# Gated cross attention with a routed layer: context rows with room for eight columns, and the turned weights in two buffers of their own

## The chip, the cores and the metric

The kernel runs on one core of a Trainium2 chip. The metric is the device time of one execution in microseconds (us); less is better. The time of a version is the median of its runs.

## The reference

`x` is (32, 112, 512), the context `ctx_2048` is (32, 375, 512), all fp32. For each of the 32 batches the kernel computes one head of attention over the context, and then every token goes to the one of eight experts that a router picks.

```python
def attend(h, memory, mask):                  # (B,112,512), (B,375,512), (B,375)
    scores = einsum('bsd,bmd->bsm', h, memory) / sqrt(512)
    scores = where(mask[:, None, :], scores, -1e30)
    return einsum('bsm,bmd->bsd', softmax(scores), memory)   # 0 where no row is valid

def routed(x, Wg, W, b):
    probs = softmax(x @ Wg)                   # 8 experts
    e = argmax(probs)
    return probs[e] * (x @ W[e] + b[e])

x = x + tanh(g_xattn) * attend(layernorm(x), ctx_2048, mask)
x = x + tanh(g_ffn) * routed(layernorm(x), Wg, W, b)
```

## The kernel before

The work has two phases. In the **batch phase** a loop goes over the 32 batches (unrolled by four, `TURN = 4`), software pipelined: each engine's program for step i works on several batches at once. In the **tail phase** 35 tiles of 128 tokens, sorted by expert, are gathered, multiplied with their expert's matrix and scattered to the output.

*Layout.* The 375 rows of a context are put on 125 partitions (`MP`), three rows each (`MC = 3`): partition p holds rows 3p, 3p+1 and 3p+2, which adjoin in DRAM. In SBUF they lie in `ctx_sb`, shape (128, 12, 632): four slots (batches j, j+1, j+2, j+3) of three chunks, and each chunk has `SE + D` = 120 + 512 columns. The 512 are the context row. The 120 (`SE`) are in front of it, for the turned softmax weights: `S` = 112 columns for the tokens of the batch and `E` = 8 for the router's part. A chunk is then, in one row of SBUF, [112 weights | 8 router values | 512 context values].

*SP (sync)* issues the loads. In `batch(i)` (line 393) it waits for `w_lo_ok`, loads a piece of the expert matrices (`load_w`, line 373), waits for `x2_ok` of batch i, stores batch i's rows to DRAM (`mid_rows`, line 398) and issues `load(i + 4)`: x (line 366), then the context in two DMAs, partitions 0 to 111 (line 368) and 112 to 124 (line 369). Both count on one semaphore per slot, `ctx_ld`.

*TensorE (PE)* goes in step i, in this order (`batch`, line 1193): scores of batch i+1 (lines 1104 to 1108, the last being the mask matmul); the turn (transpose) of the softmax weights of batch i into `prob_ps` (`turn_weights`, line 1116); the turn of the context of batch i+2, quarters 0 and 1 (`ctx_turn`, line 1082), which waits for that batch's load; the router's ranks of batch i-2 (lines 1127 and 1128); the first third of the read-out of batch i (`read_out`, lines 1141 and 1142), the one that waits for `prT_ok`; the turn of x of batch i+2 (line 1091) and of the context's quarters 2 and 3; the other two thirds of the read-out. One third of a read-out is a matmul with 125x112 weights and 8 + 256 moving columns, and one with the other 256. The eight columns are the router's part, which the matmul multiplies with the softmax weights in the same pass.

*ScalarE (ACT)* goes in step i (`batch`, line 698): `apply1` (line 695), a small exponential for the router (line 712), `turned_weights` (line 680), then the copies of the turned context quarters out of PSUM (`ctx_part`, lines 630 and 632), of the turned x (line 687), of a piece of the matrices (line 742), and the softmax exponential (line 665).

*VectorE (DVE)* subtracts for the low parts of the fp32 split (lines 968 and 1053), takes the statistics of x of batch i+3 (`stats1`, line 769, which waits for that load), writes x2 (`residual`, line 824) and does the router's small steps. `read_counts` (line 942) reads a count that PE puts in unused columns of `prob_ps`, so it waits for `prT_ok` too.

*Tail phase.* `ctx_sb`'s 512-column parts are used again: eight chunks for the biases, four for the results (line 253), which GpSimd scatters (line 590).

`prT_ok` counts the copies of the turned weights, one a batch; `read_mm` counts finished read-outs.

Of the kernel before, what the change touches and what calls it, by code (L numbers as in the profile page):

```python
# [24 lines left out]
ACT = mybir.ActivationFunctionType  # L25
AX = mybir.AxisListType

P = 128
# [62 lines left out]
def loop_end(last):  # L91

    return (last - 4) // TURN * TURN
# [14 lines left out]
def build(nc, x, ctx, mask, small, w_exp, b_exp, out):  # L108
    B, S, D = x.shape
    M = ctx.shape[1]  # L110
    E = b_exp.shape[0]
    N = B * S
    KC = D // P
    MC = 3
    MP = M // MC

    MAIN = MP // 16 * 16
    ME = M + M % 2

    SE, MG = S + E, ME + E  # L120
# [3 lines left out]
    HALF = D // 2  # L124
# [7 lines left out]
    TAIL = loop_end(B + 2)  # L132
# [13 lines left out]
    with ExitStack() as stack:  # L146
        def sb(name, shape, dt=F32):
            return stack.enter_context(nc.sbuf_tensor(name, shape, dt))

        def ps(name):  # L150
            return stack.enter_context(nc.psum_tensor(name, [P, 512], F32))

        def sem(name):
            return stack.enter_context(nc.semaphore(name))


        ident = sb("ident", [P, P])
# [17 lines left out]
        late = w_lo[:, (B - 2) * D:B * D]  # L175
# [11 lines left out]
        gv = sb("gv", [P, B])  # L187

        x_sb = sb("x_sb", [P, 4, D])
        ctx_sb = sb("ctx_sb", [P, 4 * MC, SE + D])  # L190
        xn = sb("xn", [S, D])
        xnT_hi = sb("xnT_hi", [P, KS, SE], F32R)
        xnT_lo = sb("xnT_lo", [P, KS, SE], F32R)
# [56 lines left out]
        put = sb("put", [P, 4], U32)  # L250


        rows, biases, res = x_sb, ctx_sb[:, 0:E, SE:], ctx_sb[:, E:E + 4, SE:]
        rn = w_raw
        rnT_hi, rnT_lo = (part[:, :, :].rearrange("p k m -> p (k m)")[:, 0:2 * D].rearrange("p (a d) -> p a d", a=2)
                          for part in (ctxT_hi, ctxT_lo))
# [4 lines left out]
        read_a, read_b = read_both[0:S, 512 - HALF - E:512], read_both[0:S, 512:512 + HALF]  # L261
        read_ps, pg_ps = read_both[0:S, 512 - HALF:512 + HALF], read_both[0:S, 512 - HALF - E:512 - HALF]
        prob_ps = ps("prob_ps")
# [10 lines left out]
        def chunks(j):  # L274
            return slice(MC * j.slot(4), MC * j.slot(4) + MC)
# [6 lines left out]
        ctx_ld = [sem(f"ctx_ld{i}") for i in range(4)]  # L282
# [21 lines left out]
        prT_mm, prT_ok, read_mm = sem("prT_mm"), sem("prT_ok"), sem("read_mm")  # L304
# [59 lines left out]
        def _(sp):  # L364
            def load(j):
                sp.dma_start(x_sb[0:S, j.slot(4), :], x_rows[bass.ds(j.times(S), S), :]).then_inc(x_ld[j.slot(4)], 16)
                rows_of = ctx[bass.ds(j.times(1), 1), :, :].rearrange("o (p c) d -> p (o c) d", c=MC)
                sp.dma_start(ctx_sb[0:MAIN, chunks(j), SE:], rows_of[0:MAIN, :, :]).then_inc(ctx_ld[j.slot(4)], 16)
                sp.dma_start(ctx_sb[MAIN:MP, chunks(j), SE:], rows_of[MAIN:MP, :, :]).then_inc(ctx_ld[j.slot(4)], 16)

            def load_w(w):

# [245 lines left out]
        def _(act):  # L618
# [56 lines left out]

            def turned_weights(j):
                act.wait_ge(prT_mm, j.times(1, 1))
                if j.at_least(4):
                    act.wait_ge(read_mm, j.times(1, -3))
                act.activation(ctx_sb[0:MP, chunks(j), 0:SE],  # L680
                               prob_ps[0:MP, 0:MC * SE].rearrange("p (c s) -> p c s", c=MC), ACT.Copy).then_inc(prT_ok, 1)

            def turned_x(j):
                act.wait_ge(xnT_mm, j.times(1, 1))
# [68 lines left out]
        def _(dve):  # L753
# [187 lines left out]

            def read_counts(late):
                dve.wait_ge(count_mm, late + 1)
                dve.wait_ge(prT_ok, B if late else TAIL + 1)
                dve.tensor_scalar(cnt_i[:, :], count_ps, float(P - 1) if late else 0.0, None, ALU.add
                                  ).then_inc(count_ok, 1)
                dve.wait_ge(count_ok, 2 * late + 1)
                dve.tensor_scalar(til_i[:, :], cnt_i[:, :], 7, None, ALU.arith_shift_right).then_inc(count_ok, 1)
# [121 lines left out]
        def _(pe):  # L1070
            def ctx_turn(j, k):

                if k == 0:
                    pe.wait_ge(ctx_ld[j.slot(4)], j.rounds(4) * 32 + 32)
                if k >= 2:
                    pe.wait_ge(ctxT_ok, j.times(KS, k - 1))
                elif k == 1 and j.at_least(1):
                    pe.wait_ge(ctxT_full_ok, j.times(1))
                elif j.at_least(1):
                    pe.wait_ge(ctxT_ok, j.times(KS))  # L1080
                for c in range(MC):
                    last = pe.transpose(ctx_ps[k % 2][:, c * MP:(c + 1) * MP],  # L1082
                                        ctx_sb[0:MP, MC * j.slot(4) + c, SE + k * P:SE + (k + 1) * P], ident[0:MP, 0:MP])
                    if c == MC - 1:
                        last.then_inc(ctxT_mm, 1)

# [43 lines left out]
            def read_out(j, c):  # L1130
                a = j.slot(2)
                if c == 0:
                    pe.wait_ge(prT_ok, j.times(1, 1))
                    if j.at_least(1):
                        pe.wait_ge(x2_ok, j.times(1))
                        pe.wait_ge(lg_ok, j.times(1))
                    else:
                        pe.wait_ge(gv_ok, 1)

                turned = ctx_sb[0:MP, MC * j.slot(4) + c, :]  # L1140
                pe.matmul(read_a, turned[:, 0:S], turned[:, S:SE + HALF], start=(c == 0), stop=(c == MC - 1))  # L1141
                last = pe.matmul(read_b, turned[:, 0:S], turned[:, SE + HALF:], start=(c == 0), stop=(c == MC - 1))  # L1142
                if c == MC - 1:
                    last.then_inc(read_mm, 1)

# [159 lines left out]
```

## Time and profile before

| | us |
|---|---|
| median of 3 runs | 391.55 (391.52 to 391.95) |
| the profiled execution | 394.58 |
| its span, first to last instruction | 392.8 |
| PE busy | 359.2 (91%) |
| weight loads (PEld) busy | 302.1 (77%) |
| DVE busy | 301.0 (77%) |
| GpSimd (POOL) busy | 226.8 (58%) |
| ACT busy | 220.6 (56%) |
| HBM read, written | 51.68 MB, 17.10 MB |
| DMA packets | 39438, 67.21 MB |

A profile is one execution. Matmuls are pipelined, and their ends are modelled, so a busy PE need not be at its peak. The idle time of an engine is put down to whatever released it. The chain of waits is followed back from the last instruction, at each step to what released it; it shows which work ended last. The mean granted clock of TensorE is 0.976.

### The profile page before, as it was taken

The page shows a single profiled execution, that of the slowest core. Times are in us where ns is not written, and L with a number is a line of the kernel's source. Part 1 is how long each engine was busy: PE and PEld are TensorE (multiplying, and loading weights), DVE is VectorE, ACT ScalarE, POOL GpSimd, SP SyncE. Part 2 cuts the span into 40 slices and gives each one's busy share as a digit, 9 for nine tenths or more (in the row PEclk, how much of TensorE's full clock was granted, in tenths as well). Part 3 has the DMA queues.
Part 4 walks back from the last instruction along what each step waited for, and adds up shares of the span by engine and source line. Part 5 has one row for each costly group of instructions (what it writes and reads, how often), then busy time and mean ns, then how long its engine had stood idle before and what let it go on. Part 6 is the DMA issues. An engine that isn't in the chain of part 4 may idle for free.

```text
span 392.8 us, 9753 instructions
## 1 busy us (share of the span) xinstructions
PE 359.2 (91%) x2062; PEld 302.1 (77%) x2063; DVE 301.0 (77%) x1087; ACT 220.6 (56%) x488; POOL 226.8 (58%) x482
## 2 busy tenths in 40 slices
PE   7799999999999999999999999376999999999980
PEld 6688888878888888888888877255777878878760
DVE  4668888889898899889899988446877767767660
ACT  3577777777777677767777665132434444444410
POOL 5154675665666666665675654726466666666631
PEclk9999999999999999999999999968999999999995
DMA  7978789888989888899999861754345444445410
GB/s 197 222 188 222 179 196 221 194 199 204 202 203 197 206 193 217 201 188 220 198 201 234 196 152 52 164 179 135 110 158 158 141 146 145 129 149 158 153 37 0
DMA packets 39438, 67.21 MB, mean 171 GB/s; under 512 B 10578, under 2 KB 11094, under 8 KB 39416
## 3 DMA queue, kind: packets, MB, share of 16 engines
q1 hardware_dynamic: 32600, 50.35, 54.7%
q0 software_dynamic: 6624, 16.58, 13.2%
q8 instruction: 8, 0.13, 0.1%
q14 instruction: 14, 0.11, 0.1%
q10 hardware_dynamic: 192, 0.03, 0.0%
HBM read 51.68 MB, written 17.10 MB: 175 GB/s over the span
## 4 chain that ended last, share of the span: by engine, by line
PE 52%; DMA 16%; issue 9%; DVE 7%; POOL 6%; ACT 3%; SPq 3%; POOLq 1%; DVEq 1%; ACTq 0%
DMA ctx_sb<-in_ctx 8%; PE read_both L1141 8%; PE ctx_ps L1082 8%; PE read_both L1142 7%; DMA x_sb<-mid_rows,take 6%; PE score_ps L1180 4%; PE score_ps L1107 3%; POOL out_rows L590 3%; PE score_ps L1182 3%; PE score_ps L1181 3%; PE score_ps L1104 3%; PE score_ps L1105 3%; PE score_ps L1106 3%; PE prob_ps L1091 2%; PE ctx_ps L1162 2%
## 5 line engine op out<-in xcount | busy, mean ns | idle before, releaser
L1141 PE MATMUL read_both<-ctx_sb 125*112 125x264 f32 x192 | 61.1, 400 | 1.9 <-DVE lg L837 1.6
L1180 PE MATMUL score_ps<-w_hi,ctxT_hi 128*128 x140 | 59.7, 426 | 1.6 <-DVE ctxT_lo L908 1.6
L968 DVE TENSOR_TENSOR ctxT_lo<-ctx_ps,ctxT_hi 128x375 fp32r<-128x375 f32 x96 | 49.3, 541 | 13.2 <-ACT ctxT_hi L630 12.6
L520 POOL DMA_INDIRECT token_list<-pay,pos x32 | 32.2, 1007 | 46.2 <-DVE pos L889 41.1
L1142 PE MATMUL read_both<-ctx_sb 125*112 125x256 f32 x192 | 57.1, 379 | 0.0
L1082 PE MATMUL ctx_ps<-ident,ctx_sb 125*128 125x125 f32 x384 | 52.6, 272 | 4.4 <-DMA ctx_sb<-in_ctx 2.6
L1182 PE MATMUL score_ps<-w_lo,ctxT_hi 128*128 x140 | 56.4, 403 | 0.0
L1181 PE MATMUL score_ps<-w_hi,ctxT_lo 128*128 x140 | 56.3, 402 | 0.0
L581 POOL DMA_INDIRECT x_sb<-mid_rows,take x35 | 34.4, 982 | 29.8 <-DVE ctx_sb L926 17.9
L590 POOL DMA_INDIRECT out_rows<-ctx_sb,put x35 | 40.0, 1144 | 17.5 <-issue 9.4
L641 ACT ACTIVATE w_raw<-x_sb,li 128x512 f32<-128x512 f32 x35 | 28.5, 815 | 36.9 <-DMA x_sb<-mid_rows,take 36.9
L1082 PEld LDWEIGHTS ctx_ps<-ident,ctx_sb 125*128 125x128 f32 x384 | 42.4, 141 | 7.0 <-DMA ctx_sb<-in_ctx 2.7
L630 ACT ACTIVATE ctxT_hi<-ctx_ps 128x375 fp32r<-128x375 f32 x96 | 42.6, 481 | 4.9 <-PE ctx_ps L1082 4.9
L695 ACT ACTIVATE xn<-x_sb,ln 112x512 f32<-112x512 f32 x32 | 26.0, 814 | 33.3 <-POOL ln L484 33.3
L654 ACT ACTIVATE ctxT_hi<-ctx_ps 128x512 fp32r<-128x512 f32 x35 | 20.9, 598 | 40.6 <-PE ctx_ps L1162 40.6
L469 POOL TENSOR_TENSOR w_lo<-w_raw,w_hi 128x512 f32 (+1 forms) x32 | 40.8, 1275 | 0.0
L1142 PEld LDWEIGHTS read_both<-ctx_sb 125*112 125x112 f32 x192 | 34.0, 177 | 8.7
L1104 PE MATMUL score_ps<-ctxT_hi,xnT_hi 128*120 128x384 f32 x96 | 37.9, 395 | 1.8 <-DVE ctxT_lo L968 1.8
L921 DVE SCALAR_TENSOR_TENSOR x_sb<-ctx_sb,li,x_sb 128x512 f32<-128x512 f32 x35 | 26.3, 752 | 13.1 <-issue 12.8
L908 DVE TENSOR_TENSOR ctxT_lo<-ctx_ps,ctxT_hi 128x512 fp32r<-128x512 f32 x35 | 24.2, 691 | 15.1 <-ACT ctxT_hi L654 15.0
L1141 PEld LDWEIGHTS read_both<-ctx_sb 125*112 125x112 f32 x192 | 29.3, 176 | 5.3 <-ACT ctx_sb L680 2.3
L926 DVE SCALAR_TENSOR_TENSOR ctx_sb<-score_ps,li,x_sb 128x512 f32<-128x512 f32 x35 | 26.3, 751 | 8.7 <-PE score_ps L1182 7.7
(141 smaller groups left out, 828.2 us busy)
## 6 DMA issues: line engine op xcount, KB each, us to landing
ctx_sb<-in_ctx SPq DMA_DIRECT2D x32, 672.0 KB
w_raw<-in_L_ffn_W SPq DMA_DIRECT2D x32, 256.0 KB, 5.1
x_sb<-in_x SPq DMA_DIRECT2D x32, 224.0 KB, 4.4
mid_rows<-x SPq DMA_DIRECT2D x32, 224.0 KB, 3.4
ctx_sb<-in_ctx SPq DMA_DIRECT2D x32, 78.0 KB
ctx_sb<-in_L_ffn_b SPq DMA_DIRECT2D x8, 256.0 KB, 7.6
li<-token_list SPq DMA_DIRECT2D x35, 2.0 KB, 1.9
x_sb<-mid_rows,take POOLq DMA_INDIRECT x35, 3.4
```

What stands on the lines that cost most here:

```text
L469: pool.tensor_tensor(w_lo[:, bass.ds(w.times(D), D)], w_raw[:, w.slot(2), :], w_hi[:, bass.ds(w.times(D), D)].bitcast(F32), ALU.subtract). ...
L581: pool.indirect_dma_start(rows[:, b, :], None, source, bass.IndirectOffsetOnAxis(take[:, b:b + 1], 0)).then_inc(row_ld[b], 16)
L590: pool.indirect_dma_start(out, bass.IndirectOffsetOnAxis(put[:, b:b + 1], 0), res[:, b, :], None, bounds_check=N - 1, oob_is_err=False).th ...
L630: act.activation(ctxT_hi[:, k, 0:M], ctx_ps[k % 2][:, 0:M], ACT.Copy).then_inc(ctxT_hi_ok, 1)
L968: dve.tensor_tensor(ctxT_lo[:, k, 0:M], ctx_ps[k % 2][:, 0:M], ctxT_hi[:, k, 0:M].bitcast(F32), ALU.subtract).then_inc(ctxT_ok, 1)
L1082: last = pe.transpose(ctx_ps[k % 2][:, c * MP:(c + 1) * MP], ctx_sb[0:MP, MC * j.slot(4) + c, SE + k * P:SE + (k + 1) * P], ident[0:MP, 0:MP])
L1104: pe.matmul(score_ps[a][0:SE, 0:MG], xnT_hi[:, k, :], ctxT_hi[:, k, :], start=(k == 0), stop=False)
L1141: pe.matmul(read_a, turned[:, 0:S], turned[:, S:SE + HALF], start=(c == 0), stop=(c == MC - 1))
L1142: last = pe.matmul(read_b, turned[:, 0:S], turned[:, SE + HALF:], start=(c == 0), stop=(c == MC - 1))
L1180: pe.matmul(y_ps[a][:, :], hi, w_hi[:, chunk], start=(k == 0), stop=False)
L1181: pe.matmul(y_ps[a][:, :], lo, w_hi[:, chunk], start=False, stop=False)
L1182: last = pe.matmul(y_ps[a][:, :], hi, w_lo[:, chunk], start=False, stop=(k == KC - 1))
```

## The change

The context is given to the kernel with 8 (`E`) columns of zeros ahead of each row, so a row in DRAM has 520 columns, 2080 B; this is done on the host. `ctx_sb` has 520 columns a chunk: [8 router values | 512 context values]. A load writes all 520, so that the three rows of a partition are 1560 adjoining values on both sides, 6240 B. The router's values are written over the eight zeros later.

The 112 columns of turned weights move to a new tile, `turned`, with two buffers. `turned_weights` makes two copies in place of one: 125 x (3 x 112) to `turned`, and 125 x (3 x 8) to `ctx_sb`. `prT_ok` counts both, so that its waits ask for twice as much; the wait for `read_mm`, from the third batch on, asks for all read-outs but that of the batch just before. The read-out takes its weights from `turned` and its moving columns from `ctx_sb`. All other users of `ctx_sb` change their offset only.

```diff
@@ buffers
-        ctx_sb = sb("ctx_sb", [P, 4 * MC, SE + D])
+        ctx_sb = sb("ctx_sb", [P, 4 * MC, E + D])
+        turned = sb("turned", [P, 2, MC * S])
...
-        rows, biases, res = x_sb, ctx_sb[:, 0:E, SE:], ctx_sb[:, E:E + 4, SE:]
+        rows, biases, res = x_sb, ctx_sb[:, 0:E, E:], ctx_sb[:, E:E + 4, E:]
@@ sync, load(j)
-                sp.dma_start(ctx_sb[0:MAIN, chunks(j), SE:], rows_of[0:MAIN, :, :]).then_inc(ctx_ld[j.slot(4)], 16)
-                sp.dma_start(ctx_sb[MAIN:MP, chunks(j), SE:], rows_of[MAIN:MP, :, :]).then_inc(ctx_ld[j.slot(4)], 16)
+                sp.dma_start(ctx_sb[0:MAIN, chunks(j), :], rows_of[0:MAIN, :, :]).then_inc(ctx_ld[j.slot(4)], 16)
+                sp.dma_start(ctx_sb[MAIN:MP, chunks(j), :], rows_of[MAIN:MP, :, :]).then_inc(ctx_ld[j.slot(4)], 16)
@@ scalar, turned_weights(j)
                 act.wait_ge(prT_mm, j.times(1, 1))
-                if j.at_least(4):
-                    act.wait_ge(read_mm, j.times(1, -3))
-                act.activation(ctx_sb[0:MP, chunks(j), 0:SE],
-                               prob_ps[0:MP, 0:MC * SE].rearrange("p (c s) -> p c s", c=MC), ACT.Copy).then_inc(prT_ok, 1)
+                if j.at_least(2):
+                    act.wait_ge(read_mm, j.times(1, -1))
+                both = prob_ps[0:MP, 0:MC * SE].rearrange("p (c s) -> p c s", c=MC)
+                act.activation(turned[0:MP, j.slot(2), :].rearrange("p (c s) -> p c s", c=MC), both[:, :, 0:S], ACT.Copy
+                               ).then_inc(prT_ok, 1)
+                act.activation(ctx_sb[0:MP, chunks(j), 0:E], both[:, :, S:SE], ACT.Copy).then_inc(prT_ok, 1)
@@ vector, read_counts(late)
-                dve.wait_ge(prT_ok, B if late else TAIL + 1)
+                dve.wait_ge(prT_ok, 2 * (B if late else TAIL + 1))
@@ tensor, ctx_turn(j, k)
-                                        ctx_sb[0:MP, MC * j.slot(4) + c, SE + k * P:SE + (k + 1) * P], ident[0:MP, 0:MP])
+                                        ctx_sb[0:MP, MC * j.slot(4) + c, E + k * P:E + (k + 1) * P], ident[0:MP, 0:MP])
@@ tensor, read_out(j, c)
-                    pe.wait_ge(prT_ok, j.times(1, 1))
+                    pe.wait_ge(prT_ok, j.times(2, 2))
...
-                turned = ctx_sb[0:MP, MC * j.slot(4) + c, :]
-                pe.matmul(read_a, turned[:, 0:S], turned[:, S:SE + HALF], start=(c == 0), stop=(c == MC - 1))
-                last = pe.matmul(read_b, turned[:, 0:S], turned[:, SE + HALF:], start=(c == 0), stop=(c == MC - 1))
+                weight, values = turned[0:MP, a, c * S:(c + 1) * S], ctx_sb[0:MP, MC * j.slot(4) + c, :]
+                pe.matmul(read_a, weight, values[:, 0:E + HALF], start=(c == 0), stop=(c == MC - 1))
+                last = pe.matmul(read_b, weight, values[:, E + HALF:], start=(c == 0), stop=(c == MC - 1))
@@ host, kernel(**inputs)
+        if name == "ctx_2048":
+            room = inputs["L0_ffn_b"].shape[0]
+            a = _np.concatenate([_np.zeros(a.shape[:2] + (room,), a.dtype), a], axis=2)
```

## Rows read from the trace of the kernel before

**Rows 1.** Page, busy times; window 27.5 to 225.1 us, engines in that order.

```profile
PE 359.2 (91%) x2062; PEld 302.1 (77%) x2063; DVE 301.0 (77%) x1087; ACT 220.6 (56%) x488; POOL 226.8 (58%) x482
...
27.50:225.10 197.60, 195.78 (x1215) 170.28 (x1213) 176.03 (x719) 142.74 (x350) 124.27 (x323) 1.00 0.88 204
```

**Rows 2.** Chain of waits, 100 to 132 us: start us, us, what.

```profile
101.16 0.16 PE score_ps L1108
101.32 0.32 PE prob_ps L1116 x3
101.64 0.64 PE ctx_ps L1082 x6
...
102.34 0.56 PE read_both L1141 x2
102.90 0.43 PE read_both L1142 x2
...
104.36 0.45 PE read_both L1141 x2
...
108.33 0.16 PE score_ps L1108
...
115.59 0.16 PE score_ps L1108
```

**Rows 3.** Instructions of line 1108 on PE, 27 to 226 us.

```profile
L1108 PE MATMUL score_ps<-mask_add,ident_bf x28: 322/322/323, 27.5 to 225.1; 128*112 128x375 bf16 x28
```

**Rows 4.** Timeline of ACT, then of the weight loads, 101 to 103 us.

```profile
101.68 0.47 ACT L680 ACTIVATE ctx_sb<-prob_ps 125x360 f32<-125x360 f32 x1
102.05 0.85 ACT L630 ACTIVATE ctxT_hi<-ctx_ps 128x375 fp32r<-128x375 f32 x2
...
102.20 0.27 PEld L1141 LDWEIGHTS read_both<-ctx_sb 125*112 125x112 f32 x2
```

**Rows 5.** Groups of ACT by form: line, shapes, count | busy us, mean ns | idle.

```profile
L630 ACT ACTIVATE ctxT_hi<-ctx_ps 128x375 fp32r<-128x375 f32 x96 | 42.6, 481 | 4.9 <-PE ctx_ps L1082 4.9
...
L654 ACT ACTIVATE ctxT_hi<-ctx_ps 128x512 fp32r<-128x512 f32 x35 | 20.9, 598 | 40.6 <-PE ctx_ps L1162 40.6
...
L687 ACT ACTIVATE xnT_hi<-prob_ps 128x336 fp32r<-128x336 f32 x32 | 14.4, 451 | 25.9 <-PE prob_ps L1091 25.9
L712 ACT ACTIVATE lexp<-lsh,pay 112x8 f32<-112x8 f32 x32 | 9.3, 290 | 3.7 <-DVE lsh L862 3.7
```

**Rows 6.** DMA queues in windows 118.5:119.5, 300:380 and 27:225 us.

```profile
DMA packets 176, 0.36 MB, mean 360 GB/s; under 512 B 0, under 2 KB 0, under 8 KB 176
...
q1 hardware_dynamic: 176, 0.36, 100.0%
...
q0 software_dynamic: 3840, 11.28, 43.6%
...
q1 hardware_dynamic: 21714, 40.22, 87.7%
```

**Rows 7.** Timeline of SP's queue, 78 to 87 us: start us, us.

```profile
78.59 0.33 SPq L366 DMA_DIRECT2D x_sb<-in_x  x1
79.12 0.64 SPq L368 DMA_DIRECT2D ctx_sb<-in_ctx  x1
79.95 0.89 SPq L369 DMA_DIRECT2D ctx_sb<-in_ctx  x1
```

**Rows 8.** Waits of PEld, 27 to 226 us, then of DVE, 20 to 226 us.

```profile
PEld ctx_ps L1082 <- DMA ctx_sb<-in_ctx: 2.7, 5, 1.0
...
DVE st L769 <- DMA x_sb<-in_x: 1.3, 4, 0.5
```

**Rows 9.** Chain of waits, the context loads on it: start us, us, what.

```profile
2.03 6.01 DMA ctx_sb<-in_ctx
...
8.18 0.53 PE ctx_ps L1082 x3
...
79.95 7.12 DMA ctx_sb<-in_ctx
...
131.44 6.57 DMA ctx_sb<-in_ctx
```
## The prediction, made before the change was run

> **What bounds the kernel now.** I read the profile from coarse to fine: the shares of busy time, one steady stretch, the chain of waits over a few batches, the waits of TensorE's weight loads, then the DMA issues and landings. The sum below is made against one profiled execution: 394.58 us with a span of 392.8 us, which is 3.0 us above the 391.55 us median of the plain runs. I add the difference that I find to the median.
>
> TensorE (PE) is busy 91% of the span and ScalarE (ACT) 56%; from 27.5 to 225.1 us, where 27 batches pass, PE is busy 195.8 of 197.6 us at a granted clock of 1.00, while the 16 DMA engines are busy 88% at 204 GB/s [rows 1]. So two resources are nearly full at once. The chain of waits says which one ends last: between the mask matmuls of two neighbouring batches, from 101.16 to 108.33 us, it stays on PE throughout, and the period is 7.17 us; the next is 7.26 us [rows 2]. The mask matmul runs once a batch, 28 times from 27.5 to 225.1 us [rows 3]: 27 periods in 197.6 us, mean 7.32. Against the undisturbed 7.17 (193.6 us) that leaves 4.0 us lost in the stretch. That 4.0 us, and what the first load costs, is all that faster context loads can give back.
>
> Within a clean batch there is one place where PE waits on ACT. Its first pair of read-out matmuls (line 1141) takes 0.56 us on the chain, the next pair 0.45 us [rows 2]. The time in between is ACT's copy of the turned weights (line 680): it runs 101.68 to 102.15 us and the weight load behind it starts at 102.20 us [rows 4]. So the end of that copy already sets when the read-out begins, by 0.11 us per batch, and whatever ends later there goes straight onto the period.
>
> **The change, part by part.**
>
> 1. *The copy is split in two (ACT).* Today one copy of 125x360; then one of 125x336 into `turned` and one of 125x24 into `ctx_sb`, and PE waits for both (the count asked for is 2j+2). Price from the copies of the profile: 128x375 takes 481 ns, 128x512 takes 598 ns [rows 5], so 0.85 ns a column and 161 ns fixed. That gives 448 ns for 336 columns (line 687, with 336 columns, shows 451 [rows 5]) and 181 ns for 24. ACT overlaps neighbours: line 680 starts at 101.68 and runs 0.47, line 630 starts at 102.05, an overlap of 0.10 us [rows 4]. So the first copy ends 20 ns sooner and the second 80 ns after it: the weights are ready 60 ns later. The upper end is the small exponential of line 712 (112x8, 290 ns [rows 5]): 290 - 100 - 20 = 170 ns later. The lower end is 0.03 us; nothing or a gain is excluded, since a second instruction has to end after the first. I take 0.07 us, near the copies, which are the same kind of operation. PE waits at that place in about 30 of the 32 batches: +2.1 us (ends +0.9 and +5.1). ACT itself has room (142.7 us busy of 197.6 [rows 1]), and the copies of `ctx_ps` behind it slip by the same 0.07 us together with the PE work that needs them.
>
> 2. *The wait for `read_mm` becomes j-1 for j-3.* ACT has already waited for the turn of the weights of batch j, which PE issues after all read-outs of j-1. So the wait is always met: cost nothing; behind it stand the copies of `ctx_ps`, and they lose nothing.
>
> 3. *The context load.* Today 375 pieces of 2048 B a batch (112 and 13 partitions, three rows each), 23.4 for each of 16 DMA engines. After, a partition's three rows adjoin on both sides, one piece of 6240 B: 125 pieces, 7.8 for each engine, and 1.6% more bytes. In the fullest microsecond of a batch 176 packets of 2 KB pass in 16 engine-microseconds, 91 ns each, or 22.5 B/ns [rows 6]. If all of that were per packet, 15.6 fewer packets would save 1.4 us of a batch; if all of it were per byte, the load would take 0.03 us more. The row to decide between these ends is the gather and scatter queue of the tail: 3840 packets with a mean of 2.9 KB, 11.28 MB in 43.6% of 16 x 80 us, which is 20.2 B/ns [rows 6]. Its larger packets are no cheaper per byte than 22.5, so the part per packet is small. I take 0.2 us earlier, nearer the lower end, and keep both ends for the range. That the mean over the steady stretch is much worse (40.22 MB in 87.7% of 16 x 198 us, 14.5 B/ns [rows 6]) says that most of the time is waiting of another kind, and there the size of a piece may or may not help.
>
>  Here the Trainium skill speaks against the change: "DMA: Bandwidth & Descriptors", section "How a descriptor splits into AXI transactions", says that a read which does not start on a 256 B boundary fetches from the boundary below, and that those bytes cost beats. By that rule 6240 B rows, whose starts are spread over the multiples of 32 B, would cost 3.5 beats of 32 B on the mean over their 195, where today's reads start aligned: the load would then grow by 3.4% and not 1.6%, an estimate, and the sum would be 0.04 us a batch worse. No row of the trace shows a misaligned read from memory.
>
> 4. *SP's issue.* The main context issue takes 0.64 us for 336 pieces, the x issue 0.33 us for 112 [rows 7]. With 112 pieces it should take about 0.34, so SP is 0.3 us ahead for the tail issue (0.89 us today [rows 7]). The tail's packets stand behind those of the main load, so I count nothing for it. The weight load after it waits for GpSimd's subtraction, not for SP.
>
> 5. *What an earlier landing is worth.* In the steady stretch weight loads of line 1082 wait 2.7 us for context, in 5 places, and VectorE waits 1.3 us for x, in 4 [rows 8]. The other waits for context are nil because the loads arrive just in time: issue to landing takes 6 to 7 us of a 7.17 us period (6.01 at the start, 7.12 and 6.57 later [rows 9]). 0.2 us earlier gives 0.2 at each of the 5 places, 1.0 us; the x loads stand behind the weight load of the batch before, so some of it reaches them too: 0.2 us; and the first load, which nothing covers (landing 8.04, first turn 8.18 [rows 9]), gives 0.2 us. Sum -1.4 us. Ends: 0.03 us later at the same places, +0.2 us; and all of it back, -4.0 and some 0.8 at the start, -4.8.
>
> 6. *Tail phase.* Biases and results sit in `ctx_sb` at another pitch; the same rows of 2 KB are read and written. Nothing.
>
> Sum: +2.1 - 1.4 = +0.7 us, 392.3 us (395.3 for a profiled execution like that of before).
>
> **The rivals.**
>
> *Slower: the second copy is not a cheap follower.* Place: between the turn of the weights and the first read-out. Price: 0.17 us a batch, as line 712 has it, x 30 = +5.1, less 1.2 of part 5: 395.5 us. It decides from 0.1 us a batch on. For it: PE already waits exactly here. Against: the copies from PSUM follow a straight line in the number of columns down to 336.
>
> *Faster: the long pieces take most of the waiting out of the queue.* If context lands 0.8 us earlier, all 4.0 us of the steady stretch and 0.8 of the start come back: -4.8 + 2.1 = -2.7, 388.9 us; with 0.5 us it is about 389.8. For it: 14.5 against 22.5 B/ns, so there is waiting to remove. Against: the packets of the fullest microsecond show no cost that a longer piece would spare [rows 6], and the waiting between them need not come from their size.
>
> *Slower: odd starts make the loads longer.* Landings have little margin, so 0.25 us more would stall most batches, by perhaps 0.15 us each: +4.1 + 2.1, 397.7 us. This is the direction in which the skill's rule on 256 B points, but its own 0.04 us a batch would give only 1.1 us in 27 batches.
>
> *The change does not do what it says:* if the pieces stay one row each (2080 B), the load is 1.6% longer and only ACT's cost remains: 393.8 us.
>
> **How the numbers follow.** 0.2% is 0.8 us, about what a measurement of this kernel can tell from no change: faster is below 390.8, slower above 392.3. Forecast case (cost and gain nearly cancel, 391.2 to 393.2): 0.42. Faster rival: 0.25. Dear copy: 0.17. Longer loads: 0.08. No longer pieces: 0.08. Faster than 0.2%: 0.24 of the faster rival and 0.04 of the forecast case, 0.28. Within: 0.25 of the forecast case and 0.05 of the others, 0.30. Slower: 0.42. The forecast's own number stands at the edge of two of these. The range goes from 389.0 (nearly all of the faster rival) to 395.8 (the dear copy in it); it leaves out the longer loads and the last of the faster rival.
>
> **What would show it.** In the profile after: a first copy of about 448 ns and a second of 180 to 200 ns, the weight load of the read-out 0.05 us behind the end of the second, and clean periods of 7.22 to 7.25 us for 7.17. About 8,000 packets fewer on the hardware queue with 1% more bytes. Context landing 0.2 us sooner after its issue than in the rows of before, SP's main issue near 0.34 us. Waits for context in the steady stretch of about 1.5 us for 2.7. I am wrong if the clean period doesn't move (the copy is hidden), if it moves by over 0.12 us, or if the landing moves by over 0.5 us either way.

## The result, and the profile after

The changed kernel takes 394.5 us (median of 6 runs, 393.35 to 395.95) against 391.53 us before: ratio 1.0076, 95% interval 1.0043 to 1.0109. It is slower by 3.0 us.

The profiled executions don't show it: 394.83 us after and 394.58 us before, spans 393.0 and 392.8 us. The one of before lay 3 us above its median, so what it lost in waits must be weighed with care. But the two traces show clearly what changed.

The page and the window of the same 27 batches, from the mask matmul of batch 2 to that of batch 29 (29.7 to 225.4 us here), columns as in [rows 1]:

```profile
PE 360.8 (92%) x2062; PEld 304.4 (77%) x2063; DVE 300.0 (76%) x1087; ACT 222.6 (57%) x520; POOL 226.8 (58%) x482
...
29.70:225.40 195.70, 195.70 (x1215) 171.32 (x1213) 175.09 (x719) 144.29 (x377) 124.29 (x323) 1.00 0.83 208
```

PE is busy without a gap: 195.7 of 195.7 us, where it had 195.8 of 197.6. 27 periods take 195.7 us for 197.6. The chain of waits over three batches, start, length and what, against [rows 2]:

```profile
102.33 0.16 PE score_ps L1111
...
103.51 0.62 PE read_both L1144 x2
...
105.59 0.45 PE read_both L1144 x2
...
109.57 0.16 PE score_ps L1111
...
116.85 0.16 PE score_ps L1111
```

The period without a stall, the clean period, is 7.24 us for 7.17 (the smallest distance of two mask matmuls in the window is 7.23 for 7.16). The first pair of read-out matmuls takes 0.62 us where it took 0.56, the next pair 0.45 as before. ACT's timeline and the weight loads at that place, against [rows 4]:

```profile
102.85 0.45 ACT L682 ACTIVATE turned<-prob_ps 125x336 f32<-125x336 f32 x1
103.19 0.18 ACT L684 ACTIVATE ctx_sb<-prob_ps 125x24 f32<-125x24 f32 x1
103.26 0.87 ACT L631 ACTIVATE ctxT_hi<-ctx_ps 128x375 fp32r<-128x375 f32 x2
...
103.43 0.27 PEld L1144 LDWEIGHTS read_both<-ctx_sb,turned 125*112 125x112 f32 x2
```

The first copy takes 0.45 us and would let the read-out begin at 103.35. The second begins at 103.19, ends 185 ns later, at 103.38, and the weight load follows at 103.43, 0.05 us behind it.

The queues of the page and of the window 29 to 227 us, and SP's issues, against [rows 6, 7]:

```profile
DMA packets 15955, 40.98 MB, mean 207 GB/s; under 512 B 2927, under 2 KB 2927, under 8 KB 15944
...
q1 hardware_dynamic: 15112, 40.82, 82.2%
...
87.99 0.32 SPq L369 DMA_DIRECT2D ctx_sb<-in_ctx  x1
88.50 0.32 SPq L370 DMA_DIRECT2D ctx_sb<-in_ctx  x1
```

6,600 packets fewer carry 1.5% more bytes in 82.2% of the engines' time for 87.7%: 15.7 B/ns for 14.5. SP's context issues take 0.32 us each for 0.64 and 0.89. The context itself lands, by the trace's landing records, a median of 6.9 us after its main issue, for 7.2. The waits for context of [rows 8] are gone from this window, and the wait for x too.

The start tells the other half. Chain of waits, 0 to 18 us, against [rows 9]:

```profile
1.26 6.25 DMA small_sb<-in_small
...
7.54 0.22 DVE wg_part L786
...
8.67 1.18 PE score_ps L1267 x16
9.85 1.25 PE ctx_ps L1085 x6
...
16.33 0.16 PE score_ps L1111
```

Before, the chain ran through the first context load, which landed at 8.04 us. Now it runs through `small_sb`, the 17 KB of router weights and gates that ACT loads at the same time. Landing of that load before, and after:

```profile
DMA to landing us min/median/max: 2.6/2.6/2.6
...
DMA to landing us min/median/max: 6.3/6.3/6.3
```

It was issued at 1.3 us in both. From 1.5 to 5.5 us its queue's packets took 5.4% of the engines' time, for 4.8%, which is 0.2 us for each engine in both: the 3.7 us more lie between the packets, not in them. PE's program has the router's sum ahead of the first turn of a context, and the sum needs this load. The context itself landed at 7.7 us, but its first turn began at 9.64 us (8.18 before), and the first mask matmul came at 16.17 us for 14.03. TensorE stood idle for 2.4 us meanwhile, and its granted clock fell. PE's timeline at the router's sum, then windows of before and after, granted clock third from the end:

```profile
7.89 0.36 PE L1255 MATMUL small_ps<-wg_part,w_lo 128*128 128x8 f32 x2 [2.39 <-DVE wg_part L786]
...
8.00:14.00 6.00, 4.47 (x27) 3.64 (x28) 2.93 (x7) 2.53 (x6) 1.75 (x9) 1.00 0.90 233
...
8.00:16.20 8.20, 7.33 (x48) 6.38 (x49) 4.36 (x17) 3.29 (x7) 1.49 (x9) 0.79 0.67 170
```

So from trace to trace: +2.1 us at the start, +1.9 in 27 batches from the copies, -3.8 from stalls that are gone (what 27 periods take above 27 clean ones: 4.2 us before, with 7.16 us as the clean one, and 0.4 now). That makes +0.2 us, as the two spans have it, and not the +3.0 us of the medians.

The page's DMA issues, KB and median us to landing:

```profile
w_raw<-in_L_ffn_W SPq DMA_DIRECT2D x32, 256.0 KB, 4.6
x_sb<-in_x SPq DMA_DIRECT2D x32, 224.0 KB, 3.9
mid_rows<-x SPq DMA_DIRECT2D x32, 224.0 KB, 2.9
```

Before they took 5.1, 4.4 and 3.4 us. Each lands 0.5 us sooner after its issue, though only the context's pieces were changed. They stand in the same queue as the context; whether the longer pieces or the longer period shortened it, these two traces can't tell (see e1 and e5).

### The profile page after: what moved, and what is told of

Same layout as the page of the kernel before. It is cut to its first block, busy times and chain, and to the rows that moved or that the text cites. A ratio compares the mean times of both kernels' runs of the same rounds, so it can differ in the third digit from the quotient of the medians.

```text
span 393.0 us, 9811 instructions
## 1 busy us (share of the span) xinstructions
PE 360.8 (92%) x2062; PEld 304.4 (77%) x2063; DVE 300.0 (76%) x1087; ACT 222.6 (57%) x520; POOL 226.8 (58%) x482
## 4 chain that ended last, share of the span: by engine, by line
PE 80%; DMA 7%; DVE 4%; issue 3%; ACT 2%; POOL 1%; DVEq 0%; POOLq 0%; SPq 0%; ACTq 0%
PE read_both L1144 12%; PE ctx_ps L1085 10%; PE read_both L1145 10%; PE score_ps L1183 7%; PE score_ps L1185 6%; PE score_ps L1184 6%; DMA x_sb<-mid_rows,take 5%; PE score_ps L1110 5%; PE score_ps L1107 4%; PE score_ps L1108 4%; PE score_ps L1109 4%; PE ctx_ps L1165 3%; PE prob_ps L1094 3%; PE prob_ps L1119 3%; DMA small_sb<-in_small 2%
## 5 line engine op out<-in xcount | busy, mean ns | idle before, releaser
L1144 PE MATMUL read_both<-ctx_sb,turned 125*112 125x264 f32 x192 | 61.1, 400 | 1.8 <-DVE lg L840 1.5
L1145 PE MATMUL read_both<-ctx_sb,turned 125*112 125x256 f32 x192 | 57.1, 379 | 0.0
L1085 PEld LDWEIGHTS ctx_ps<-ident,ctx_sb 125*128 125x128 f32 x384 | 43.7, 144 | 2.4 <-DVE ctxT_lo L971 1.6
L1145 PEld LDWEIGHTS read_both<-ctx_sb,turned 125*112 125x112 f32 x192 | 34.0, 177 | 8.7
L1144 PEld LDWEIGHTS read_both<-ctx_sb,turned 125*112 125x112 f32 x192 | 29.2, 176 | 5.3 <-ACT ctx_sb L684 2.4
```

The source lines that it names most:

```text
L1085: last = pe.transpose(ctx_ps[k % 2][:, c * MP:(c + 1) * MP], ctx_sb[0:MP, MC * j.slot(4) + c, E + k * P:E + (k + 1) * P], ident[0:MP, 0:MP])
L1144: pe.matmul(read_a, weight, values[:, 0:E + HALF], start=(c == 0), stop=(c == MC - 1))
L1145: last = pe.matmul(read_b, weight, values[:, E + HALF:], start=(c == 0), stop=(c == MC - 1))
```

## The experiments

They ran on two other chips, e1 to f1 and b0 on one, a0 and g1 to g3 on the other. The kernel before takes 395.65 and 395.78 us on the first of these (35 and 29 runs) and 395.84 on the second (35 runs), 392.7 to 404.0 in all. A single time spreads by 1% there, so I go by intervals for times and by the traces for mechanisms. "First mask" is the start of the first mask matmul; the clean period is the smallest distance of two such matmuls; the excess is what 27 periods, from batch 2 to 29, take above 27 clean ones. The small load is that of `small_sb`. Warming matmuls multiply ones with ones into a place that nobody reads, to keep TensorE busy.

| kernel | ratio to before, 95% | small load lands | first mask | clean period | excess |
|---|---|---|---|---|---|
| before (b0) | - | 3.9 | 14.30 | 7.17 | 5.7 |
| changed (a0) | 1.0027 (0.9992 to 1.0063) | 7.1 | 16.73 | 7.23 | 1.8 |
| e1 short pieces | 1.0017 (0.9988 to 1.0047) | 3.8 | 14.54 | 7.23 | 2.4 |
| e2 small load first | 1.0001 (0.9974 to 1.0028) | 2.7 | 15.91 | 7.23 | 2.4 |
| e3 values first | 0.9989 (0.9959 to 1.0019) | 7.4 | 16.16 | 7.15 | 3.0 |
| e4 both | 0.9948 (0.9922 to 0.9974) | 2.8 | 18.23 | 7.15 | 3.3 |
| e5 before, two copies | 1.0048 (1.0015 to 1.0080) | 3.8 | 15.33 | 7.23 | 2.9 |
| e8 e5, values first | 1.0016 (0.9983 to 1.0049) | 3.9 | 13.96 | 7.15 | 6.1 |
| f1 e4, warming | 0.9983 (0.9947 to 1.0019) | 2.9 | 14.12 | 7.15 | 4.2 |
| g1 first load short | 0.9976 (0.9947 to 1.0004) | 3.8 | 14.51 | 7.23 | 7.1 |
| g2 g1, values first | 0.9973 (0.9938 to 1.0008) | 3.8 | 14.57 | 7.15 | 3.5 |
| g3 warming in the wait | 1.0054 (1.0021 to 1.0087) | 7.3 | 15.00 | 7.23 | 3.3 |

The last four columns (us) are of the one profiled execution. The kernel before has no profile on the chip of a0 and g1 to g3.

**e1, short pieces.**

```diff
-                sp.dma_start(ctx_sb[0:MAIN, chunks(j), :], rows_of[0:MAIN, :, :]).then_inc(ctx_ld[j.slot(4)], 16)
-                sp.dma_start(ctx_sb[MAIN:MP, chunks(j), :], rows_of[MAIN:MP, :, :]).then_inc(ctx_ld[j.slot(4)], 16)
+                sp.dma_start(ctx_sb[0:MAIN, chunks(j), E:], rows_of[0:MAIN, :, E:]).then_inc(ctx_ld[j.slot(4)], 16)
+                sp.dma_start(ctx_sb[MAIN:MP, chunks(j), E:], rows_of[MAIN:MP, :, E:]).then_inc(ctx_ld[j.slot(4)], 16)
```

> The changed kernel, but the loads leave out the eight zero columns, so that the pieces are one row of 2048 B each again (from and into the padded layout). Everything else, the two copies too, is as changed. Nothing reads the eight columns before they are written. Theory: the changed kernel lost about 2.1 us at the start, because the router weights' small packets share the DMA engines packet by packet with 6240 B pieces and land at 7.5 us instead of 3.8, and about 0.07 us a batch by the second copy; it won back the few stalls for context. With short pieces the small load should land before 4.5 us, the first mask matmul come back to 14.1 us (16.2 as changed), the clean period stay 7.23 to 7.25 us, and some waits for context return. Time 2 us above before (0.5%). Rival A, that the padded layout or the pitch delays the start: the small load stays at 6 us or later. Rival B, that only the copies cost: the same time as changed, +3.0 us.

The small load landed 2.5 us after its issue and the first mask came at 14.54 us, with the padded layout, the two copies and `turned` all in place. So the long pieces alone delay the small load, and rival A falls. The period stayed at 7.23. The excess is 2.4 us, more than the 0.4 us of the first profile of the changed kernel, but e2, with long pieces, the same period and the same chip, has 2.4 us too: at this period the two profiles show no use of the long pieces for the stalls. The time was 0.17% above before, less than the 0.5% expected.

**e2, small load first on SP's queue.**

```diff
-            act.dma_start(small_sb[:, :], small).then_inc(small_ld, 16)
...
+            sp.dma_start(small_sb[:, :], small).then_inc(small_ld, 16)
             load(Count(0))
```

> The changed kernel with the small load (router weights and gates) issued by SP ahead of the first x load, and no longer by ACT beside it; long pieces kept. Theory: standing first in the same queue it lands before 4.5 us; the first turn of the context then waits for the context load alone (landing near 8.1 us, since SP is 0.5 us later) and the first mask matmul comes at 14.2 to 14.5 us for 16.2. Time 1.7 to 2.1 us below the changed kernel, about 1 us above before (+0.2 to +0.4%). Rival A (padded layout delays the start in another way): no gain over the changed kernel, +0.7 to +0.8%. Rival B (only the copies cost): no gain either.

The load landed early, at 2.7 us, and the first turn came at 8.21 us, right behind the context. But the first mask was late all the same, at 15.91 us. PE's timeline before that turn, and windows:

```profile
8.21 1.14 PE L1085 MATMUL ctx_ps<-ident,ctx_sb 125*128 125x125 f32 x6 [1.24 <-DMA ctx_sb<-in_ctx]
...
8.00:16.00 8.00, 7.07 (x28) 6.14 (x29) 3.12 (x7) 3.20 (x6) 1.45 (x9) 0.57 0.93 240
```

PE waited 1.24 us for the context, and from 8 to 16 us its mean granted clock was 0.57. A matmul on the chain of the first scores took 0.32 us there for 0.18. So the expected first mask matmul (14.2 to 14.5 us) was missed: an early landing of the small load is not enough, if TensorE then stands idle before the context and its clock falls. The interval of the time (0.9974 to 1.0028) holds no change and the lower end of what was expected.

**e3, values first.** The wait for the second copy moves behind the matmul that doesn't need it.

```diff
-                    pe.wait_ge(prT_ok, j.times(2, 2))
+                    pe.wait_ge(prT_ok, j.times(2, 1))
...
-                pe.matmul(read_a, weight, values[:, 0:E + HALF], start=(c == 0), stop=(c == MC - 1))
-                last = pe.matmul(read_b, weight, values[:, E + HALF:], start=(c == 0), stop=(c == MC - 1))
+                pe.matmul(read_b, weight, values[:, E + HALF:], start=(c == 0), stop=(c == MC - 1))
+                if c == 0:
+                    pe.wait_ge(prT_ok, j.times(2, 2))
+                last = pe.matmul(read_a, weight, values[:, 0:E + HALF], start=(c == 0), stop=(c == MC - 1))
```

> The changed kernel with the read-out's two matmuls of a third in the other order: first the 256 columns that need only the turned weights, behind a wait for the first copy alone (2j+1), then the eight router columns and the other 256, behind the wait for the second copy. Theory: PE's wait at this place ends with the first copy, 20 ns before where it ended in the kernel before and 80 ns before where it ends as changed, so the clean period falls from 7.23 to about 7.15 us, and 30 batches give 2.1 to 2.7 us below the changed kernel, +0.1 to +0.2% against before; the late start at 16.2 us stays. Rival (the period grew for another reason, such as the weights' or the values' new place in SBUF, or the copies behind the second one being late): the period stays at 7.23 and the time at +0.7 to +0.8%.

```profile
102.00 0.16 PE score_ps L1111
...
109.16 0.16 PE score_ps L1111
...
102.52 0.45 ACT L682 ACTIVATE turned<-prob_ps 125x336 f32<-125x336 f32 x1
102.87 0.19 ACT L684 ACTIVATE ctx_sb<-prob_ps 125x24 f32<-125x24 f32 x1
...
103.02 0.27 PEld L1144 LDWEIGHTS read_both<-ctx_sb,turned 125*112 125x112 f32 x2
```

The first copy ends at 102.97 us and the weight load starts at 103.02, before the second copy's end at 103.06. The period fell to 7.16 us here, 7.15 at its smallest. So the second copy was the whole growth of the period, and the rival falls. The late start stayed. Against the changed kernel (a0, 1.0027, another chip) the point is 1.5 us lower, for 2.1 to 2.7 expected, and the intervals overlap.

**e4, both.** The diffs of e2 and e3 together.

> Both edits together: small load first on SP's queue, and the values' matmul first behind the first copy. Theory: the gains add, since one is at the start and one in each batch: 4 to 4.8 us below the changed kernel, which is 1 to 1.8 us below before (-0.25 to -0.5%). Rival: with a period of 7.15 us the context loads are late again and stalls for them take up to 1.5 us of it back, time equal to before within 0.2%.

Ratio 0.9948: 2.1 us faster than before, the only version whose interval lies below 1. That it is the one of eleven, and that f1, which holds both of its edits, comes to 0.9983, are reasons to take the size with care. Its profiled execution was its slowest (398.1 us for a median of 393.75), so it shows only how bad the start can get: context landing at 9.55 us, 2.81 us idle, clock 0.53 from 8 to 16 us, first mask at 18.23.

**e5, the kernel before with two copies.**

```diff
-                act.activation(ctx_sb[0:MP, chunks(j), 0:SE],
-                               prob_ps[0:MP, 0:MC * SE].rearrange("p (c s) -> p c s", c=MC), ACT.Copy).then_inc(prT_ok, 1)
+                both = prob_ps[0:MP, 0:MC * SE].rearrange("p (c s) -> p c s", c=MC)
+                act.activation(ctx_sb[0:MP, chunks(j), 0:S], both[:, :, 0:S], ACT.Copy).then_inc(prT_ok, 1)
+                act.activation(ctx_sb[0:MP, chunks(j), S:SE], both[:, :, S:SE], ACT.Copy).then_inc(prT_ok, 1)
...
-                dve.wait_ge(prT_ok, B if late else TAIL + 1)
+                dve.wait_ge(prT_ok, 2 * (B if late else TAIL + 1))
...
-                    pe.wait_ge(prT_ok, j.times(1, 1))
+                    pe.wait_ge(prT_ok, j.times(2, 2))
```

> The kernel before, its layout and its 2048 B pieces kept, with ScalarE's copy of the turned weights split in two (112 and 8 columns of each chunk) and all waits asking for both. Theory: only the price of the second copy: weights ready 60 to 70 ns later, clean period 7.23 us for 7.16, and 1.0 to 2.1 us more in all, less where a stall for context takes the longer period up; the start stays where the kernel before has it (first mask matmul near 14.0 to 14.5 us). Time +0.2 to +0.5% against before. Rival: the second copy alone costs nothing and the period grew by the new place of weights and values: period 7.16, time as before.

```profile
29.05 0.16 PE score_ps L1109
...
36.28 0.16 PE score_ps L1109
...
43.52 0.16 PE score_ps L1109
```

7.23 and 7.24 us, with the old layout and the weights in their old place: the rival falls, and the copy's price stands alone. 0.48% is 1.9 us, at the upper end of what was expected. Its start was at 15.33 us with a clock of 0.79 from 8 to 16 us, so the fallen clock is not peculiar to the long pieces. One more thing stands in its profile: with the old layout and the old pieces the excess is 2.9 us for 5.7 in b0, on the same chip, and PEld waits 1.6 us for context for 4.3. So with no change to the loads, and a period longer by 0.06 us that gives each of them that much more time, about half of the stalls are gone, as far as one profile each can show it.

**e8, e5 with the values first.** The diff of e3 on e5.

> The kernel before with the two copies of the experiment beside it, and the values' 256 columns multiplied first, behind the first copy alone; pieces of 2048 B kept. Theory: clean period 7.15 us, start as before. What is left against the version with long pieces is the stalls for context: with a period at least as short as before and the same loads I expect 3 to 6 us of stalls over 27 batches, so the time is -0.1 to +0.1% against before. Rival: the long pieces are of no use to the stalls, then this one is as fast as the best version with long pieces.

Period 7.15 us and excess 6.1, near the 3 to 6 us expected: with short pieces a period that short is mostly lost again to the loads. PEld waited 3.8 us for context and DVE 3.9 us for x between 27 and 226 us. The four profiles with long pieces and the same period lose 3.0 (e3), 3.3 (e4), 4.2 (f1) and 3.5 us (g2, another chip). That is the use of the long pieces, some 2 to 3 us, as far as one profile each can show it; at 7.23 us e1 and e2 show none. The times (1.0016 against 0.9989, 0.9948, 0.9983 and 0.9973) point the same way, but only e4's interval is apart from this one's.

**f1, e4 with more warming.**

```diff
-    WARM, WARM_MORE = 40, 16
+    WARM, WARM_MORE = 40, 40
```

> The changed kernel with the small load first on SP's queue, values' matmul first behind the first copy, and 40 warming matmuls in place of 16 between the router's sum and the first turn of the context (1.6 us more of work on TensorE, at a place where it has nothing else to do). In the two runs with the small load first, TensorE was idle for 1.2 and 2.8 us before the first context landed, and the granted clock fell to 0.50 until about 15 and 18 us. Theory: kept busy up to the landing it holds the clock at 1.00, and the first mask matmul comes at 14.1 to 14.7 us for 15.9 and 18.2. Time 1.5 to 3.5 us below the same kernel without the warming, -0.9 to -1.3% against before. Rival: the clock falls anyway or the context lands at 9.5 us again, and the gain is under 0.5 us.

```profile
8.00:16.00 8.00, 6.19 (x47) 5.08 (x45) 3.61 (x9) 4.15 (x9) 1.60 (x9) 1.00 0.99 247
```

The clock held at 1.00 and the first mask came at 14.12 us, as expected. Its time didn't follow: 0.9983, above e4's 0.9948 where it should lie 1.5 us or more below. Its twelve runs go from 391.96 to 396.86 us, a spread like that of the others. A part of such a spread can stand in the tail phase, which none of the experiments edits: from the last mask matmul to the end f1 and e5 took 148.1 us, all other profiles 149.8 (g3) to 151.2. Windows of before, e5 and f1:

```profile
250.00:280.00 30.00, 19.01 (x82) 14.70 (x81) 15.60 (x59) 8.26 (x16) 14.49 (x20) 0.83 0.51 159
...
250.00:280.00 30.00, 19.51 (x90) 15.02 (x89) 16.05 (x67) 8.66 (x17) 15.80 (x23) 0.89 0.57 158
...
250.00:280.00 30.00, 19.77 (x91) 15.04 (x89) 17.77 (x66) 9.52 (x17) 16.73 (x21) 0.89 0.57 174
```

At the handover to the tail phase the granted clock was 0.89 in these two and 0.83 or less in all the others. These 2.4 us are as large as anything that the experiments are after, and whether they come and go between executions of one kernel is not known, with one profile of each.

**b0, the kernel before beside e1 to f1.**

> The kernel before, unchanged, for a profile on the chip of the other runs. Theory: clean period 7.16 us, small load landing before 4.5 us, first mask matmul at 14.0 to 14.6 us, and some 3 to 6 us lost over 27 batches to waits for context or x. Rival: this chip's start is slower in the kernel before as well (first mask matmul after 15 us), and that is why its runs here take 395.7 us and not 391.5.

```profile
PEld ctx_ps L1082 <- DMA ctx_sb<-in_ctx: 4.3, 7, 1.1
...
14.30 0.32 PE L1108 MATMUL score_ps<-mask_add,ident_bf 128*112 128x375 bf16 x1
```

The start is as in the first profile, so the rival falls; PEld waits 4.3 us for context in 7 places, where [rows 8] have 2.7 in 5, and the excess is 5.7 us for 4.2. The loads and the store of the page land 5.3, 4.5 and 3.9 us after issue, for 5.1, 4.4 and 3.4 in the first profile, which a kernel with just-in-time loads pays for.

**a0, the changed kernel again.** It ran with g1 to g3, on the third chip, and not beside b0.

> The changed kernel, unchanged, on the chip of the experiments, where the kernel before takes 395.7 us. Theory: two costs, +2.1 us in the 30 batches and +1.5 to +2.1 us at the start (small load landing near 7.5 us for 3.9, first mask matmul near 16.2 us), less the stalls of the kernel before, which are larger on this chip (5.6 us in its profile here over 27 batches, 4.2 us in the first profile; 0.4 us in the changed one): +0.1 to +0.8% against before. Rival: the same ratio as at first, +0.76%, whatever the stalls of the kernel before are here.

1.0027, where the first chip gave 1.0076 with an interval that doesn't reach it; the costs in the trace are the same (small load 5.9 us after issue, first mask 16.73, period 7.23). The two intervals overlap, so the two ratios need not differ at all. It fits the theory that the gain depends on how much the kernel before loses to its loads (excess 5.7 in b0 against 1.8 here, on two chips), but is no proof of it.

**g1, first load short.** The pieces of e1 for batch 0 alone.

```diff
-                sp.dma_start(ctx_sb[0:MAIN, chunks(j), :], rows_of[0:MAIN, :, :]).then_inc(ctx_ld[j.slot(4)], 16)
-                sp.dma_start(ctx_sb[MAIN:MP, chunks(j), :], rows_of[MAIN:MP, :, :]).then_inc(ctx_ld[j.slot(4)], 16)
+                at = E if j.turn is None and j.at == 0 else 0
+                sp.dma_start(ctx_sb[0:MAIN, chunks(j), at:], rows_of[0:MAIN, :, at:]).then_inc(ctx_ld[j.slot(4)], 16)
+                sp.dma_start(ctx_sb[MAIN:MP, chunks(j), at:], rows_of[MAIN:MP, :, at:]).then_inc(ctx_ld[j.slot(4)], 16)
```

> The changed kernel with the pieces of the first context load alone back at one row of 2048 B (its eight zero columns are left out; nothing reads them before they are written); the other 31 loads keep 6240 B. It undoes the change at the one place that I hold for the delayed start. Theory: small load landing below 4.5 us, first mask matmul at 14.0 to 14.8 us, period 7.23 us: 1.5 to 2.1 us below the changed kernel. Rival (the start is slow for another reason, such as the clock alone): first mask matmul still after 15.5 us.

```profile
DMA to landing us min/median/max: 2.5/2.5/2.5
...
14.51 0.32 PE L1112 MATMUL score_ps<-mask_add,ident_bf 128*112 128x375 bf16 x1
```

One load of 32 undone and the whole delay is gone: the place is the first load. 0.9976 against a0's 1.0027 is 2.0 us, as expected, though the intervals (up to 1.0004, and from 0.9992) just overlap. (Its profiled execution has one batch of 11.01 us in it; nothing but the start is read from it.)

**g2, g1 with the values first.**

> The same with the values' 256 columns multiplied first behind the first copy. Both costs are then undone and the long pieces kept for 31 loads. Theory: first mask matmul at 14.0 to 14.8 us, period 7.15 us, 2.4 us below the run beside it less 0.5 to 1.5 us of stalls that come back with the shorter period; against before -0.3 to -0.8%. Rival: the stalls take back all of it, and it is as fast as before within 0.2%.

0.9973: against the changed kernel 2.1 us less, against g1 no gain that can be told. Start 14.57 us, period 7.15, excess 3.5. Against before the expectation (-0.3 to -0.8%) is just missed, and the interval (0.9938 to 1.0008) doesn't part it from the rival.

**g3, warming while the small load is out.**

```diff
-    WARM, WARM_MORE = 40, 16
+    WARM, WARM_MORE = 76, 16
```

> The changed kernel with 76 in place of 40 warming matmuls ahead of the router's sum, 2.4 us more of work in the 2.4 us in which TensorE waits for the small load. It parts the start's cost into the late landing and the fallen clock. Theory: the landing stays at 7.5 us, the granted clock stays at 1.00 from 8 to 16 us (0.79 as changed), and the first mask matmul comes at 15.2 to 15.7 us for 16.2: 0.5 to 1.0 us of the 2.1 us was the clock. Rival: the clock falls all the same, or the landing alone makes up the 2.1 us: first mask matmul at 16.1 us or later.

```profile
8.00:16.00 8.00, 7.27 (x44) 6.58 (x44) 4.05 (x15) 3.24 (x7) 1.72 (x9) 0.59 0.75 199
...
8.00:16.00 8.00, 6.65 (x56) 5.70 (x55) 3.97 (x15) 3.48 (x8) 1.59 (x9) 1.00 0.75 194
...
15.00 0.32 PE L1111 MATMUL score_ps<-mask_add,ident_bf 128*112 128x375 bf16 x1
```

With the landing still at 7.3 us the clock stayed at 1.00 (0.59 in a0) and the first mask came at 15.00 us. On this chip that parts the delay: 16.73 us (a0), 15.00 (late landing, full clock), 14.51 (g1, early landing, full clock), so 1.7 us were the fallen clock and 0.5 the late landing, more for the clock than the 0.5 to 1.0 expected. In the first profile the clock stood lower for a shorter time (0.79 from 8 to 16 us), and its 2.1 us may part in another way.

But the time was no better: 1.0054 against a0's 1.0027, intervals overlapping. A part of that lies outside the span of the instructions: in eleven of g3's twelve runs the time is 2.4 to 2.9 us above the span, in every other kernel here 1.7 to 1.9. By the spans alone the medians are 395.2 us for g3 and 395.1 for a0. With f1 this is the second time that an earlier start, seen in a profile, didn't lower the median; why stays open.

## Why the prediction was right or wrong

The time, 394.5 us, lies in the range (389.0 to 395.8), 2.2 us above the forecast, on the slower side, which had the largest chance. That it lies there is in part luck. No case of the prediction gives 394.5 us by what the runs showed: the forecast case ends at 393.2, the case without longer pieces stands at 393.8, the dear copy at 395.5 (395.3, if the 1.4 us of part 5 are taken off and not 1.2), and the start, where the profiles differ most, had the wrong sign. None of the signs of being wrong that it names came up, since they look at the period and at the context's landing alone.

- **Part 1, the split copy: right.** Forecast 181 ns for the second copy, overlapping by 100, weights 60 ns later, period up by 0.07. Measured 185 ns; the end of the second lies 80 ns behind that of the first; period 7.16 to 7.23. e5 shows the same period with the old layout, e3 that the growth is gone when PE doesn't wait for the second copy. So the dear-copy rival was wrong.
- **Part 2: right.** No wait for `read_mm` shows in the trace.
- **Part 3, the load: right in direction.** The DMA engines' busy time fell by 6% with more bytes. Taken: 0.2 us earlier; in the first pair of profiles the context landed 0.3 us and the other loads and the store of a batch 0.5 us sooner after their issue. From b0 to a0, on two chips, the others gained 0.4, 0.1 and 0.6 us. As to the 256 B rule of the Trainium skill ("DMA: Bandwidth & Descriptors", "How a descriptor splits into AXI transactions"): by the layout the starts were spread as described, and the load as a whole got quicker. No run here shows what misaligned reads cost by themselves.
- **Part 4: half right.** The main issue took 0.32 us for the 0.34 forecast. That the tail issue would fall from 0.89 to 0.32 I hadn't seen. SP is done earlier in each batch, and what that gave the loads no run parts from the pieces themselves.
- **Part 5, the start: this step failed.** "The first load, which nothing covers (landing 8.04, first turn 8.18 [rows 9]), gives 0.2 us" looked at one load alone. Another DMA was in flight beside it, of 17 KB in small packets (192 with the mask's, 0.03 MB in all), and took 6.3 us for 2.6. TensorE waited for it, its clock fell, and the first mask matmul came 2.1 us later where 0.2 were to be gained. e1 and g1 show the cause: short pieces, for batch 0 alone even, bring the landing back to 2.5 us. The small load wasn't in my list of who shares the queue's engines, and my rival "longer loads" looked at the steady stretch.
- **Part 5, the steady waits: too small, and for one reason that I left out.** Forecast 1.2 us back; the first pair of profiles shows 3.8. But I counted the longer period as a cost and the faster loads as the only gain. In e5's profile the longer period comes with fewer stalls by itself (excess 2.9 us for 5.7 with the old pieces), and e1 and e2 are alike at 2.4. So how much of the 3.8 us the long pieces gave is not shown.
- **The base.** The profiled execution of before lay 3.0 us above its median, so in the first chip's plain runs less than its 4.2 us of stalls can have been lost. By difference (+2.1 of the start, +2.1 of the copies, +3.0 measured) 1.2 us came back there. This is arithmetic, not shown by a run, and it takes for granted that the start's 2.1 us are in the median, which f1 and g3 put in doubt. On a chip where the same kernel before takes 395.8 us, the changed one came within 0.3%.

## What to carry to other kernels

When one DMA's pieces get longer, look at every other DMA that is in flight at the same time, the smallest first: here its landing went from 2.6 to 6.3 us after issue, and at the start of a kernel nothing hides that. Split a copy so that the matmul that needs the smaller part comes last: the second instruction's tail then costs nothing (7.23 to 7.15 us a batch). Where loads arrive just in time, don't count a change of the period alone: in the profiles a longer period had fewer stalls (e5: 2.9 us for 5.7), a shorter one more (e8: 6.1). Long pieces beat the kernel before clear of noise only once (e4, 0.9948), with both of the other edits.

## What the runs showed of the hardware that I had not expected

- A small load's landing went from 2.6 to 6.3 us after issue when the pieces beside it went from 2048 to 6240 B, and back with them (2.5 us in e1 and g1). Issued first on the same queue as the long ones it landed in 1.9 us (e2).
- The granted clock after a short idle time at the start. TensorE's idle time just before the first turn of the context, and the mean granted clock from 8 to 16 us: 0.82 us and 1.00 (e8), 0.89 and 1.00 (before), 1.15 and 1.00 (b0), 1.00 and 0.79 (g2), 1.24 and 0.57 (e2), 1.58 and 0.79 (e5), 2.81 and 0.53 (e4). So the length of that gap doesn't tell by itself what the clock does: b0's 1.15 us cost nothing where g2's 1.00 did, and e5's 1.58 cost less than e2's 1.24. The level in the slow part was 0.50, that is 1.2 GHz. With the gap filled by warming matmuls it was 1.00 (f1, g3).

```profile
8.44 0.83 PE L1082 MATMUL ctx_ps<-ident,ctx_sb 125*128 125x125 f32 x6 [1.15 <-DMA ctx_sb<-in_ctx]
...
8.07 1.44 PE L1086 MATMUL ctx_ps<-ident,ctx_sb 125*128 125x125 f32 x6 [1.00 <-DMA ctx_sb<-in_ctx]
```

(PE's timelines of b0 and of g2.)

- The issue of 13 partitions took 0.89 us with three pieces each and 0.32 us with one, no more than that of 112 partitions.
- The same two kernels differed by 0.76% on one chip (391.5 us before; interval 0.43 to 1.09%) and by 0.27% on another (395.8 us; -0.08 to 0.63%). The intervals overlap.
